# Leaving the gate's product in its PSUM bank, with the rounded half copied out by ScalarE

## The reference, cut to what matters

```python
x = layernorm(x + attn(x, gamma, w_q, w_kv, w_out))     # second-order Taylor feature map of q and k
h = silu((x @ w1.T) * s1) * ((x @ w2.T) * s2)           # 128 -> 512: "the gate"
h = gelu((h @ h1.T) * hs1)                              # 512 -> 512, layer 2
h = gelu((h @ h2.T) * hs2)                              # 512 -> 512, layer 3
x = layernorm(x + (h @ w3.T) * s3)                      # 512 -> 128, layer 4
```

## Time and profile before

| | |
|---|---|
| time, median of 3 runs | 720.27 us (716.29 to 723.78) |
| span of the profiled execution | 725.5 us |
| busy: PE / DVE / ACT / POOL | 89% / 79% / 63% / 39% |
| chain that ended last: PE / DVE / issue | 54% / 22% / 16% |
| one full step | 41.0 us, in some steps about 42.5 us |

### The profile page before, as it was taken

How to read it: one execution, slowest core, us unless ns; L and a number is a source line. 1 busy time by engine, 2 the same in 40 slices (tenths; PEclk the granted TensorE clock), 3 DMA queues, 4 the chain that set the end, 5 groups by cost and what they waited for, 6 DMA issues and landing times.

```text
span 725.5 us, 13222 instructions
## 1 busy us (share of the span) xinstructions
PE 643.7 (89%) x4385; PEld 462.5 (64%) x4385; DVE 572.8 (79%) x1017; ACT 454.1 (63%) x1002; POOL 284.8 (39%) x281
## 2 busy tenths in 40 slices
PE   3474989999898999989898999989899998989985
PEld 2343667676676757666775757667675766677653
DVE  3674697978879797978979797987979797996673
ACT  3462747576585757667585857658575766647563
POOL 4944243424444343343444342444434334341000
PEclk9985999999999999999999999999999999999998
DMA  6000000000101001010100000010100100000000
GB/s 208 1 0 17 1 14 3 1 30 1 29 0 29 0 0 29 0 29 0 29 0 25 4 0 29 0 29 0 29 0 0 29 0 30 15 0 2 15 15 14
DMA packets 7225, 11.97 MB, mean 16 GB/s; under 512 B 801, under 2 KB 1825, under 8 KB 7201
## 3 DMA queue, kind: packets, MB, share of 16 engines
q1 hardware_dynamic: 7200, 11.65, 5.2%
HBM read 7.45 MB, written 4.19 MB: 16 GB/s over the span
## 4 chain that ended last, share of the span: by engine, by line
PE 54%; DVE 22%; issue 16%; POOL 3%; ACT 3%; DVEq 0%; DMA 0%; SPq 0%; POOLq 0%; ACTq 0%
PE fps L380 15%; PE fps L381 13%; DVE hid_lo L785 9%; PE acc L349 8%; PE ring L339 7%; PE ring L312 5%; DVE wide L727 4%; DVE phi_k L238 3%; PE acc L358 2%; DVE h L791 2%; PE ring L298 2%; DVE wide L725 2%; ACT gate_zo L593 2%; DVE wide L732 1%; PE ring L290 1%
## 5 line engine op out<-in xcount | busy, mean ns | idle before, releaser
L380 PE MATMUL fps<-hid_hi,w_hi 128*128 128x512 f32 x576 | 247.5, 430 | 37.1 <-DVE hid_lo L785 34.6
L381 PE MATMUL fps<-hid_lo,w_hi 128*128 128x512 f32 x576 | 232.8, 404 | 0.0
L785 DVE TENSOR_TENSOR hid_lo<-h,hid_hi 128x512 fp32r<-128x512 f32 x192 | 155.7, 817 | 28.3 <-ACT hid_hi L605 27.5
L604 ACT ACTIVATE h<-fps,col 128x512 f32<-128x512 f32 x128 | 88.1, 689 | 122.4 <-PE fps L381 114.7
L380 PEld LDWEIGHTS fps<-hid_hi,w_hi 128*128 128x128 f32 x576 | 111.8, 194 | 70.1 <-DVE hid_lo L785 47.2
L381 PEld LDWEIGHTS fps<-hid_lo,w_hi 128*128 128x128 f32 x576 | 112.0, 194 | 17.7
L544 ACT ACTIVATE phiT<-ring 128x512 f32<-128x512 f32 x160 | 94.0, 600 | 44.7 <-PE ring L339 42.8
L238 DVE TENSOR_TENSOR phi_k<-phi_k 128x1024 f32<-128x1024 f32 x64 | 105.7, 1655 | 8.6 <-ACT v_one L544 8.6
L339 PEld LDWEIGHTS ring<-const,phi_q 128*128 128x128 f32 x640 | 79.2, 144 | 39.5 <-issue 20.0
L339 PE MATMUL ring<-const,phi_q 128*128 128x128 f32 x640 | 98.0, 282 | 6.9 <-POOL phi_q L928 6.1
L928 POOL TENSOR_TENSOR phi_k<-phi_k 128x64 f32<-128x64 f32 x64 | 34.8, 543 | 162.2 <-ACT v_one L544 162.0
(11 more groups left out here) (82 smaller groups left out, 938.8 us busy)
## 6 DMA issues: line engine op xcount, KB each, us to landing
x_b<-in_x SPq DMA_DIRECT2D x16, 256.0 KB, 2.8
out<-gate_zo SPq DMA_DIRECT2D x16, 256.0 KB, 2.9
h<-in_h SPq DMA_DIRECT2D x1, 1024.0 KB, 8.4
gate_zo<-in_h SPq DMA_DIRECT2D x1, 1024.0 KB, 10.4
wide<-in_w SPq DMA_DIRECT2D x3, 256.0 KB, 4.0
w_qkv_raw<-in_w_kv SPq DMA_DIRECT2D x1, 128.0 KB, 2.5
const<-in_consts SPq DMA_DIRECT2D x1, 98.5 KB, 2.4
w_qkv_raw<-in_w_q SPq DMA_DIRECT2D x1, 64.0 KB, 2.4
```

Source lines behind the costliest of these rows:

```text
L380: nc.tensor.matmul(fps[:, bank, :], w_hi[:, o:o + P], hi, start=start, stop=False)
L381: mm = nc.tensor.matmul(fps[:, bank, :], w_hi[:, o:o + P], lo, start=False, stop=stop and not with_lo)
L604: nc.scalar.activation(h32[:, n % 4, :], fps[:, bank, :], ACT.Gelu, scale=scale)
L785: nc.vector.tensor_tensor(lo, h32[:, n % 4, :], hi.bitcast(F32), ALU.subtract).then_inc(split_ready, 1)
```

## The change

`gate_mult` writes its product back into the PSUM bank that b came from, instead of to `h32`. It no longer frees the bank; a new semaphore `prod_ready` says that the product is there. `gate_hi` moves from DVE to ACT, where it copies the bank, rounded, into `hid[0]` hi. `gate_lo` on DVE subtracts that half from the bank and frees the bank. `split_ready` counts only the tiles of layers 2 and 3, and PE waits on `f_free` of b's bank for the gate's lo halves. `h32` is used by the gelu tiles alone.

```diff
-                    if m == 0:
-                        pe.wait_ge(split_ready, 3 * KT * (t - 2) + before + k + 1)
+                    if m == 0 and layer == 0:
+                        pe.wait_ge(f_free[bank_of(FPS, f"b{k}")], read(FPS, t, f"b{k}"))
+                    elif m == 0:
+                        pe.wait_ge(split_ready, 2 * KT * (t - 2) + KT * (layer - 1) + k + 1)
...
+            def gate_hi(t, m):
+                act.wait_ge(prod_ready, KT * (t - 2) + m + 1)
+                nc.scalar.activation(hid[0][0][:, m, :], fps[:, bank_of(FPS, f"b{m}"), :], ACT.Copy)\
+                    .then_inc(hi_ready, 1)
...
             def gate_mult(t, m):
...
-                nc.vector.scalar_tensor_tensor(out=h32[:, m, :], in0=fps[:, bank_of(FPS, b), :],
-                                               scalar=s2_c[:, m:m + 1], in1=gate[:, m % 2, :], op0=ALU.mult,
-                                               op1=ALU.mult).then_inc(f_free[bank_of(FPS, b)], 1)
-
-            def gate_hi(t, m):
-                dve.wait_ge(f_free[bank_of(FPS, f"b{m}")], read(FPS, t, f"b{m}"))
-                nc.vector.tensor_copy(hid[0][0][:, m, :], h32[:, m, :]).then_inc(hi_ready, 1)
+                nc.vector.scalar_tensor_tensor(out=fps[:, b, :], in0=fps[:, b, :], scalar=s2_c[:, m:m + 1],
+                                               in1=gate[:, m % 2, :], op0=ALU.mult, op1=ALU.mult)\
+                    .then_inc(prod_ready, 1)
 
             def gate_lo(t, m):
+                bank = bank_of(FPS, f"b{m}")
                 dve.wait_ge(hi_ready, KT * (t - 2) + m + 1)
-                split(m, 0)
+                nc.vector.tensor_tensor(hid[0][1][:, m, :], fps[:, bank, :], hid[0][0][:, m, :].bitcast(F32),
+                                        ALU.subtract).then_inc(f_free[bank], 1)
```

More of the change, by code:

```diff
@@ L195, in build @@
         x1hi_ready = sem("x1hi_ready")
-        hi_ready, split_ready = sem("hi_ready"), sem("split_ready")
+        prod_ready, hi_ready, split_ready = sem("prod_ready"), sem("hi_ready"), sem("split_ready")
         zmv_ready, zveps_ready, zrstd_ready, out_ready = (
@@ L393, in layer1, with hidden @@
                         .then_inc(f_full, 1)
-            def hidden(t, what, o, wide, src, before, m, tiles, with_lo):
+            def hidden(t, what, o, wide, src, layer, m, tiles, with_lo):
                 for k in tiles:
@@ L411, in layer3 @@
             def layer3(t, m, tiles, with_lo):
-                hidden(t, f"three{m}", oh2, HID, 1, KT, m, tiles, with_lo)
+                hidden(t, f"three{m}", oh2, HID, 1, 1, m, tiles, with_lo)
             def layer4(t, tiles, with_lo):
-                hidden(t, "y", o3, D, 0, 2 * KT, 0, tiles, with_lo)
+                hidden(t, "y", o3, D, 0, 2, 0, tiles, with_lo)
             def transpose_y(t):
@@ L590, in silu @@
                 if m >= 2:
-                    act.wait_ge(f_free[bank_of(FPS, f"b{m - 2}")], read(FPS, t, f"b{m - 2}"))
+                    act.wait_ge(prod_ready, KT * (t - 2) + m - 1)
                 nc.scalar.activation(gate[:, m % 2, :], fps[:, bank_of(FPS, f"a{m}"), :], ACT.Silu,
                                      scale=s1_c[:, m:m + 1]).then_inc(f_free[bank_of(FPS, f"a{m}")], 1)
+            def gate_hi(t, m):
+                act.wait_ge(prod_ready, KT * (t - 2) + m + 1)
+                nc.scalar.activation(hid[0][0][:, m, :], fps[:, bank_of(FPS, f"b{m}"), :], ACT.Copy)\
+                    .then_inc(hi_ready, 1)
             def gelu(t, layer, m):
                 what = f"{('two', 'three')[layer]}{m}"
-                n = KT * (layer + 1) + m
+                n = 2 * KT * (t - 2) + KT * layer + m
                 act.wait_ge(f_full, written(FPS, t, what))
-                act.wait_ge(split_ready, 3 * KT * (t - 2) + n - 3)
+                if is_positive(n - 3):
+                    act.wait_ge(split_ready, n - 3)
                 scale = (hs1_c, hs2_c)[layer][:, m:m + 1]
                 bank = bank_of(FPS, what)
-                nc.scalar.activation(h32[:, n % 4, :], fps[:, bank, :], ACT.Gelu, scale=scale)
+                nc.scalar.activation(h32[:, m, :], fps[:, bank, :], ACT.Gelu, scale=scale)
                 nc.scalar.activation(hid[1 - layer][0][:, m, :], fps[:, bank, :], ACT.Gelu, scale=scale)\
@@ L624, in step @@
                     silu(t, 1)
+                    gate_hi(t, 0)
                 if front:
@@ L629, in step @@
                     silu(t, 2)
+                    gate_hi(t, 1)
                 if middle:
@@ L633, in step @@
                     silu(t, 3)
+                    gate_hi(t, 2)
                 if front:
                     copy_qkv(t, 0)
+                if ffn:
+                    gate_hi(t, 3)
                 if middle:
@@ L780, in x1_lo @@
                                         ALU.subtract).then_inc(f_free[bank], 1)
-            def split(n, dst):
-                hi, lo = hid[dst][0][:, n % KT, :], hid[dst][1][:, n % KT, :]
-                nc.vector.tensor_tensor(lo, h32[:, n % 4, :], hi.bitcast(F32), ALU.subtract).then_inc(split_ready, 1)
             def gate_mult(t, m):
-                a, b = f"a{m}", f"b{m}"
-                dve.wait_ge(f_full, written(FPS, t, b))
+                a, b = f"a{m}", bank_of(FPS, f"b{m}")
+                dve.wait_ge(f_full, written(FPS, t, f"b{m}"))
                 dve.wait_ge(f_free[bank_of(FPS, a)], read(FPS, t, a))
-                nc.vector.scalar_tensor_tensor(out=h32[:, m, :], in0=fps[:, bank_of(FPS, b), :],
-                                               scalar=s2_c[:, m:m + 1], in1=gate[:, m % 2, :], op0=ALU.mult,
-                                               op1=ALU.mult).then_inc(f_free[bank_of(FPS, b)], 1)
-            def gate_hi(t, m):
-                dve.wait_ge(f_free[bank_of(FPS, f"b{m}")], read(FPS, t, f"b{m}"))
-                nc.vector.tensor_copy(hid[0][0][:, m, :], h32[:, m, :]).then_inc(hi_ready, 1)
+                nc.vector.scalar_tensor_tensor(out=fps[:, b, :], in0=fps[:, b, :], scalar=s2_c[:, m:m + 1],
+                                               in1=gate[:, m % 2, :], op0=ALU.mult, op1=ALU.mult)\
+                    .then_inc(prod_ready, 1)
             def gate_lo(t, m):
+                bank = bank_of(FPS, f"b{m}")
                 dve.wait_ge(hi_ready, KT * (t - 2) + m + 1)
-                split(m, 0)
+                nc.vector.tensor_tensor(hid[0][1][:, m, :], fps[:, bank, :], hid[0][0][:, m, :].bitcast(F32),
+                                        ALU.subtract).then_inc(f_free[bank], 1)
             def gelu_tile(t, layer, m):
@@ L805, in gelu_tile @@
                 dve.wait_ge(f_free[bank_of(FPS, what)], read(FPS, t, what))
-                split(KT * (layer + 1) + m, 1 - layer)
+                hi, lo = hid[1 - layer][0][:, m, :], hid[1 - layer][1][:, m, :]
+                nc.vector.tensor_tensor(lo, h32[:, m, :], hi.bitcast(F32), ALU.subtract).then_inc(split_ready, 1)
             def step(t, par, front, middle, ffn, tail):
@@ L811, in step @@
                     gate_mult(t, 0)
-                    gate_hi(t, 0)
                     gate_mult(t, 1)
@@ L822, in step @@
                 if ffn:
-                    gate_hi(t, 1)
                     gate_mult(t, 2)
                     gate_lo(t, 1)
-                    gate_hi(t, 2)
                     gate_mult(t, 3)
                     gate_lo(t, 2)
-                    gate_hi(t, 3)
                     gate_lo(t, 3)
```

## The result

The changed kernel takes 770.19 us (median of 4 runs, 767.41 to 770.83) against 720.06 us (716.29 to 723.78): ratio 1.0686, 95% interval 1.0639 to 1.0733. It is 50 us slower. The forecast was 764 us, 748 to 782. The profiled executions span 765.6 us and 725.5 us, 40.1 us apart; where the other 10 us of the medians are is told under the clock.

The account below looks back on a forecast made before the run. PE was taken as the tight engine (89% busy), DVE close behind. 716.3 us without clock falls plus 35.2 (16 steps of 2.2 us) gave 751.5; eight falls added 12: 763.5, rounded 764 us, range 748 to 782.

Parts of the forecast that it names:

- The added wait: Gate: PE waits for DVE's subtraction before b2, b3, two0; two0 2.60 us late, 2.2 us per step net.
- The casts and the copies: Gate: four 505 ns casts per step off DVE, worth nothing; four 598 ns copies on ACT, covered by its waits.
- The product into PSUM: Gate: DVE's product stays 0.75 us written to PSUM; subtraction from PSUM 691 ns against 685, next to nothing.
- The second rival: Gate: DVE pays for reading and writing one bank, up to 2.1 us per step, up to 797 us; chance 0.06.
- The stop at layer 3: PE's 2.24 us stop before gelu tile 3's lo half moves with PE, stays 2.2 us, absorbs nothing.
- The fifth rival: Layer 3: its 2.24 us stop takes up the whole 2.2 us, not slower, time 720 us; chance 0.05.
- the fourth: DVE without casts and the stop at layer 3 absorb part of the loss: 730 to 750 us; chance 0.06.
- The sixth: Whole step: DVE is the true bound, 32.3 us of casts come off, 688 us; chance 0.03.
- What is queued behind: After two0: hi3 behind qkv0's copy, lo3 near 377.3, DVE's norm about 2.7 us later; covered for PE.
- The number of falls of the clock: Around the stop at layer 3: eight falls in 14 steps, 1.5 us each, 12 us in all.
- The base of the sum: Whole kernel before without falls of the clock: 725.5 less 9, built on as 716.3 us.
- The third rival: Gate: clock falls there in every step too, 14 falls besides 14 at layer 3, 793 us; chance 0.06.

Follow-up runs that it names:

- The late release alone: Kernel before, product in SBUF and cast on DVE, but b's bank freed by the subtraction instead of the product: 771.28 us, ratio 1.0693.
- the pairs of kernels without it: GpSimd's two q products cut to one head of eight: changed kernel 718.01, kernel before 681.00 us; one product moved to DVE instead: 731.10 and 693.64 us.
- ScalarE's copy alone: Kernel before with the rounded half made by ScalarE; product still goes to SBUF and frees the bank at once: 722.24 us, ratio 1.0039.
- the changed kernel with short POOL products: Changed kernel with GpSimd's two products of q cut to one head of eight from the second step on: 718.01 us.

## Why the prediction was right, and where it was off

**The added wait: right in kind and size.** Predicted starts against the product at 368.04: b2 +1.41, b3 +3.61, two0 +5.81 us. Measured against the product at 383.62: +1.40, +3.58, +5.84 us. One turn was put at 2.20 us and measured 2.18 and 2.26. The stops of PE itself were put at 0.7, 0.3 and 1.3 us: before b2 it is 0.69 and before two0 1.09, a little less; before b3 the row shows none, and the lateness is in the start. A full step was to take 43.2 us and takes 43.2. The late release alone reproduces all of it.

**The casts and the copies: right in their sum.** The two together give a ratio of 1.0039 whose interval holds 1; each by itself was not measured. ACT's copy was put at 598 ns and has a median of 609.

**The product into PSUM: right at the low end.** Line 791 of the kernel before, lines 798 and 805 of the kernel after, line 801 of the late-release kernel (duration ns min/median/max):

```profile
L791 DVE SCALAR_TENSOR_TENSOR h<-fps,col,gate_zo x64: 736/750/752, 74.6 to 698.5; 128x512 f32<-128x512 f32 x64
L798 DVE SCALAR_TENSOR_TENSOR fps<-fps,col,gate_zo x64: 748/758/760, 73.6 to 735.8; 128x512 f32<-128x512 f32 x64
L805 DVE TENSOR_TENSOR hid_lo<-fps,hid_hi x64: 678/680/692, 75.5 to 737.3; 128x512 fp32r<-128x512 f32 x64
...
L801 DVE TENSOR_TENSOR hid_lo<-h,hid_hi x64: 681/682/722, 76.4 to 742.0; 128x512 fp32r<-128x512 f32 x64
```

758 ns against 750 with the result in SBUF, and 680 for the subtraction from PSUM against 682 in the late-release kernel, which has it from SBUF and holds the bank as long. The second rival, a bank that pays for being read and written, is out. The surcharge for PSUM that the Trainium skill gives (Perfetto Trace Analysis, Optimizing Scalar/DVE Operations) does not show in the duration of these tiles, nor in how soon DVE's next instruction starts where it need not wait: behind the product 0.67 us in both kernels (368.04 to 368.71 and 383.62 to 384.29), behind the subtraction a median of 0.61 us from PSUM and 0.60 from SBUF. The estimate of 0.4 us per step had besides counted all three products in full, though they read b from PSUM in both kernels.

**The stop at layer 3: right.** It kept its 2.24 us, and the pairs of kernels without it differ by the same 37 us. The fifth rival falls by that, and the fourth, since the whole 2.2 us stay. The sixth falls by ScalarE's copy alone.

**What is queued behind: right, and without a price.** lo3 waits 2.71 us for ACT's hi3, which stands behind the copies of qkv0; PE does not wait for it.

```profile
392.12 0.69 DVE L805 TENSOR_TENSOR hid_lo<-fps,hid_hi 128x512 fp32r<-128x512 f32 x1 [2.71 <-ACT hid_hi L599]
```

**The number of falls of the clock: mis-sized.** I had taken eight falls. The profiled execution has nine in steps 2 to 15, where the one before had six. It is also the shortest of the four: the other three took 2.7 to 3.4 us longer, at mean granted clocks of 0.949 to 0.951 against its 0.957, so at 1.5 us a fall the median has about eleven. That is an estimate, since only one of the four was profiled. The three falls beyond eight make 4.5 of the 6 us between 764 and 770.

The two profiles reconcile: from the first feed-forward matmul of step 2 (71.93 us after, 72.91 before) to the start of step 16 (688.74 and 654.95) it is 616.8 us against 582.0, 34.8 more, of which 3 further falls are 4.6 and the rest, 30.2, is 2.16 in each of 14 steps; the last two steps are 6.3 longer; the start-up was 1.0 shorter. 34.8 + 6.3 - 1.0 = 40.1. The medians are 50 apart because the profiled execution before took some 7 us more than its median and the one after 2.8 us less, which by the falls would be five more and two fewer.

**The base of the sum: 2 us too low, and what seemed to confirm it a coincidence.** I took 725.5 less 9, a span, and set it beside 716.29, a time. A time is 1.8 us more than its span, so by the profile a run without falls takes 718.3 us. That runs of 716.0 to 716.3 exist all the same is a difference that no profile here shows. With this, the falls and the last steps (below), and with the start-up and a turn of 2.16 us in the 14 steps, the sum would be 763.5 + 1.8 + 4.5 + 1.9 - 1.0 - 0.6 = 770.1.

**The last steps: mis-sized by 2 us.** I gave them 2.2 each, 4.4 in all; step 16 is 2.3 us longer (36.3 against 34.0) and step 17 is 4.0 (38.3 against 34.3). Step 17 has no front and no middle to run between its ffn matmuls, and there the clock falls in the gate, for 7 us, which it does not in step 17 of the kernel before. Window of that step, and PE's rows in it:

```profile
727.20:765.60 38.40, 26.01 (x97) 18.87 (x96) 17.42 (x45) 18.76 (x30) 2.01 (x2) 0.86 0.04 14
...
732.42 0.50 PE L380 MATMUL fps<-x1T_hi,w_hi 128*128 128x512 f32 x1 [1.48 <-DVE hid_lo L805]
...
734.59 0.79 PE L380 MATMUL fps<-x1T_hi,w_hi 128*128 128x512 f32 x1 [0.97 <-DVE hid_lo L805]
```

After stops of 1.48 and 0.97 us within 3 us the matmul takes 0.79 us instead of 0.50. All four profiled kernels that have the gate's stops unchanged fall there in the last step, and none of the kernels that free the bank at once does.

**The third rival: nearly out.** The changed kernel shows no fall in the gate of a full step, and without the stop at layer 3 no full step falls at all. But the late-release kernel has one. In its step 3, behind stops of 0.79, 0.78 and 1.09 us within 6 us, the granted clock fell to 0.50 at 127.5 us:

```profile
127.37 0.70 PE L380 MATMUL fps<-hid_hi,w_hi 128*128 128x512 f32 x1 [1.09 <-DVE hid_lo L801]
...
127.00:131.00 4.00, 3.63 (x12) 3.14 (x13) 3.82 (x14) 0.84 (x5) 0.59 (x2) 0.57 0.01 4
```

So the gate's stops can bring the clock down in a full step too, in one of the 56 full steps with them that were profiled, where the rival had it in every step.

**Still open.** Why a step that has the same stop of 2.24 us at layer 3 falls in clock in nine of 14 cases after and in six before. The experiments show that all falls of the full steps but the one above go with that stop; they do not show what picks the step. In the kernel after, the steps with a fall come in twos and threes with one step without between them; what that hangs on was not tried.

## What to carry to other kernels

Count how long a PSUM bank is held, not only how much work an engine does: a bank that is freed two instructions later in its reader's list can put PE and the engine that frees it into turns, when the fixed order of each makes the next release wait for the next matmul. Moving work off a busy engine gains nothing where that engine is not what PE waits for; here the wait was for a neighbour on a shared resource, and giving one of GpSimd's products to DVE, which looked like more work for the busier engine, made the kernel 3.7% faster. When banks are few, walk the order of banks against the order of the reader's list before holding one longer.

## What the runs showed of the hardware that was not expected

- DVE's 1024-wide product with both inputs in SBUF takes 1.22 us alone and 3.02 us beside POOL's. With one POOL product of 2.03 us instead of two it is still 3.03 us: DVE seems to wait for the whole of one of POOL's instructions and only then to run. That is what the Trainium skill says of the port that the two share (SBUF — State Buffer, Terms, where it calls the pair an exclusive lock, held for the full instruction); the trace agrees, with 1.8 us lost against the 2.03 us of POOL's instruction.
- The same reading fits the whole stop at layer 3 of the kernel before, and there POOL waits too. Its first product ends at 392.21 us (2.04 us after 390.18), DVE's product at 393.29, POOL's second at 395.18 and DVE's subtraction at 395.73, each starting beside the one ahead and ending about its own length behind it. POOL's second product shows it, 3.01 us long where the first took 2.04:

```profile
392.17 3.01 POOL L238 TENSOR_TENSOR phi_q<-phi_q 128x1024 f32<-128x1024 f32 x1
```

- DVE reading and writing one PSUM bank in the same instruction costs 8 ns on 750 (L798 against L791).
- The kernel before varies by 9 us from run to run (716.0 to 725.2 in 15 of 19 runs; the other four took 727.2 to 727.8). With ten runs each, ScalarE's copy alone, which has the stop at layer 3, varies by 10 us, and the changed kernel with short POOL products, which has not, by 4.4. The falls of the clock after that stop, 1.5 us each and more or fewer of them, fit most of this spread, but the kernels with both the stop and the late release varied by only 0.7 to 3.4 us in four runs each, so this is argued and not shown.
